# Second expert layer as split products of 384 and 256 columns, the feature chains shared by VectorE and GpSimd, class weights loaded behind the experts

## What is computed

```python
# 8 experts, top 2 of the softmaxed gate; token width D=192, hidden width F=768
logits = x @ gate_w + gate_b                     # [512, 8]
h = gelu(x @ w1[e] + b1[e])                      # for each expert e, 192 -> 768
y = h @ w2[e] + b2[e]                            # 768 -> 192
out = x + sum_e comb[:, e] * y_e + feat @ out_w  # comb: normalised weights of the top 2
# feat: two numbers a token, from a chain along the 64 tokens of an image
def bk_green_diag(a):                            # a: [batch, 64]
    d[n] = a[n] - 1.0 / d[n-1]                   # forward, 63 steps, one after the other
    e[n] = a[n] - 1.0 / e[n+1]                   # the same backward
    G = 1.0 / (d + e - a)
```

## Time and profile before

| | |
|---|---|
| Median of 3 runs | 411.57 us (411.3 to 412.5) |
| Profiled execution, its own time | 411.31 us |
| Its span in the trace | 409.6 us |
| TensorE busy | 384.5 us, 94% of the span |
| VectorE busy | 250.9 us, 61% |
| ScalarE busy | 174.7 us, 43% |
| GpSimd busy | 45.6 us, 11% |

### The profile page before, as it was taken

One profiled execution on the slowest core, in us unless ns is written; L12 is line 12 of the kernel. 1 busy time (PEld: TensorE's weight loads), 2 busy tenths in 40 slices (PEclk: granted clock), 3 DMA queues, 4 the chain that ended last, 5 costly groups with the idle time before them and its releaser, 6 DMA issues.

```text
span 409.6 us, 8771 instructions
## 1 busy us (share of the span) xinstructions
PE 384.5 (94%) x3602; PEld 315.0 (77%) x3602; DVE 250.9 (61%) x728; ACT 174.7 (43%) x304; POOL 45.6 (11%) x97
## 2 busy tenths in 40 slices
PE   8999999999877899999999989999999999999993
PEld 8988878788554657565548788998999899879783
DVE  1567766603497988888444487558458206677344
ACT  1256551842455565755435635235224310551420
POOL 7130010330000000100001400000000200304003
PEclk9999999999978999999999999999999989989999
DMA  7999500000289100000003996224401000000001
GB/s 194 258 223 252 118 9 2 2 0 0 61 229 272 53 2 2 2 2 3 2 0 87 280 265 162 77 60 134 130 9 56 2 0 2 2 2 2 0 2 38
DMA packets 28725, 30.69 MB, mean 75 GB/s; under 512 B 4867, under 2 KB 24137, under 8 KB 28686
## 3 DMA queue, kind: packets, MB, share of 16 engines
q1 hardware_dynamic: 28220, 29.96, 29.1%
q10 hardware_dynamic: 306, 0.17, 0.2%
q0 software_dynamic: 160, 0.01, 0.0%
HBM read 29.73 MB, written 0.39 MB: 74 GB/s over the span
## 4 chain that ended last, share of the span: by engine, by line
PE 73%; DVE 15%; ACT 5%; issue 2%; DMA 2%; POOL 2%; SPq 0%; DVEq 0%; POOLq 0%
PE ps L1510 66%; PE ps L1514 6%; DMA front<-in_x 2%; DVE front L1170 2%; DVE front L1171 2%; PE ps L1522 2%; DVE front L1179 1%; DVE front L1181 1%; DVE front L1164 1%; DVE bn L1015 1%; POOL rstd L524 1%; ACT front L745 1%; DVE front L1166 1%; DVE xn L1030 1%; DVE mv L1018 0%
## 5 line engine op out<-in xcount | busy, mean ns | idle before, releaser
L1510 PE MATMUL ps<-halves 128*128 128x512 f32 (+2 forms) x380 | 84.1, 376 | 1.3 <-ACT front L732 1.3
L1510 PEld LDWEIGHTS ps<-halves 128*128 128x128 f32 x380 | 66.5, 188 | 13.4 <-ACT front L732 1.7
L1510 PE MATMUL ps<-wide,front 128*128 128x192 f32 x432 | 73.7, 332 | 0.0
L1510 PEld LDWEIGHTS ps<-wide,front 128*128 128x128 f32 x432 | 72.0, 194 | 1.0 <-issue 0.5
L1510 PEld LDWEIGHTS ps<-front 64*32 64x32 f32 (+3 forms) x1488 | 52.0, 134 | 21.8 <-issue 9.4
L1510 PE MATMUL ps<-front 64*32 64x64 f32 (+3 forms) x1488 | 60.7, 245 | 8.1 <-ACT front L745 3.0
L732 ACT ACTIVATE front<-ps,colc 128x512 f32<-128x512 f32 x60 | 39.6, 690 | 52.3 <-PE ps L1510 52.2
L1313 DVE SCALAR_TENSOR_TENSOR xn<-ps,small,xn 128x192 f32<-128x192 f32 x28 | 9.7, 410 | 29.7 <-PE ps L1510 29.7
L1514 PE MATMUL ps<-ident,front 128*128 128x128 f32 x144 | 21.5, 286 | 6.5 <-DVE front L1181 5.3
L1514 PEld LDWEIGHTS ps<-ident,front 128*128 128x128 f32 x144 | 16.2, 144 | 10.2 <-DVE front L1181 7.2
L1510 PE MATMUL ps<-xT,turned 128*64 128x256 f32 (+1 forms) x96 | 23.4, 482 | 0.0
(11 more groups left out here) (280 smaller groups left out, 555.5 us busy)
## 6 DMA issues: line engine op xcount, KB each, us to landing
wide<-in_w SPq DMA_DIRECT2D x8, 576.0 KB, 4.7
wide<-in_w SPq DMA_DIRECT2D x8, 384.0 KB, 5.8
wide<-in_w SPq DMA_DIRECT2D x16, 192.0 KB, 6.3
front<-in_a2w SPq DMA_DIRECT2D x5, 576.0 KB
front<-in_a1w SPq DMA_DIRECT2D x5, 384.0 KB
front<-in_x SPq DMA_DIRECT2D x3, 512.0 KB, 7.9
front<-in_w_qkv SPq DMA_DIRECT2D x2, 576.0 KB, 7.7
front<-in_a1w SPq DMA_DIRECT2D x5, 192.0 KB
```

Of the source, the lines that this page charges most:

```text
L1510: return pe.matmul(o, l, r, start=start, stop=stop)
```

## The change

1. The second layer becomes split. ScalarE writes gelu's result to a scratch tile `hraw[f]`, then copies it to a high part (`hidden_high`); VectorE makes the low part (`hidden_low`). The second-layer weights get the same (`w2_high`, `w2_low`), high and low side by side, 384 columns. TensorE does, for each of 24 pairs of token and feature tile, one product of 384 columns and one of 256 (`down_split`). Its result takes all of banks 4 to 7, so there is one place in place of two, and adding it into `xn` takes eight instructions (`expert_in`).
2. The chains are shared. Of every 9 steps VectorE does 3 and GpSimd 6 (`CH_DVE, CH_ALL = 3, 9`), for experts 0 to 5; the last 9 steps, with expert 6, are VectorE's alone. A step on GpSimd is five instructions. The features are made with expert 6, not with expert 4.
3. On VectorE, `expert_in(e-1)` now stands behind `chain_part(e)` in the same turn of the loop, and behind `chains_end` and `features` in the turn of expert 6.
4. On TensorE the gate product is made ahead of the second half of the first `up`, and the exponential of the gate ahead of all gelus on ScalarE; the transposes for `combT` and the extra products move into the first layer of expert 7.
5. The memory of `a1w` and `a2w` now holds the split operands, so the class weights are loaded behind the experts: `a1w` after the second layer of expert 6, `a2w` after that of expert 7.

The diff, cut to what decides:

```diff
+CH_DVE, CH_ALL = 3, 9
@@ SyncE
-                    sp.wait_ge(s["y_mm"], e - NSLOT + 1)
+                    sp.wait_ge(s["w2_lo"], e - NSLOT + 1)
-                if e == NSLOT - 1:
...
+            sp.wait_ge(s["y_mm"], EM - 1)
+            sp.wait_ge(s["h_lo"], NF * EM)
+            for x in range(5):
+                for c, (r0, n) in enumerate(CH):
+                    load(a1w[0:n, x, c], a["a1w"][x, r0:r0 + n], "a_in")
+            sp.wait_ge(s["y_half"], 2)
+            for x in range(5):
+                load(a2w[:, x], a["a2w"][x].rearrange("(f p) n -> p f n", p=P), "a_in")
@@ GpSimd
+            def chain_step(n):
+                last = chS[:, n - 1, :]
+                link(pool.tensor_tensor(chr_[:, 0:2], last, last, ALU.mult))
+                link(pool.tensor_tensor(chr_[:, 2:3], chr_[:, 0:1], chr_[:, 1:2], ALU.add))
+                link(pool.tensor_tensor(chr_[:, 3:4], chr_[:, 2:3], chB[:, n, 1:2], ALU.pow))
+                link(pool.tensor_tensor(chr_[:, 0:2], last, chr_[:, 3:4].to_broadcast([16, 2]), ALU.mult))
+                return pool.tensor_tensor(chS[:, n, :], chr_[:, 0:2], chB[:, n, :], ALU.add)
+            for k in range(EM - 2):
+                pool.wait_ge(s["chain_dve"], k + 1)
+                for n in range(CH_DVE, CH_ALL):
...
+                tell(ins, "chain_pool")
@@ ScalarE
+            for e in range(EM):
+                for f in range(NF):
+                    expert_hidden(e, f)
+                    if f >= 1:
+                        hidden_high(e, f - 1)
+                hidden_high(e, NF - 1)
+                if e >= 1:
+                    w2_high(e)
                 if e + 2 < EM:
                     w1_high(e + 2)
@@ VectorE
+            def chain_part(e):
+                if e >= 1:
+                    dve.wait_ge(s["chain_pool"], e)
+                steps_here = CH_DVE if e < EM - 2 else CH_ALL
...
+            def expert_in(e):
+                dve.wait_ge(s["y_mm"], e + 1)
+                for i in range(NT):
+                    ins = weighted(xn, xn, e, i, 0)
+                link(ins)
+                for i in range(NT):
+                    ins = weighted(xn, xn, e, i, 1)
+                ins.then_inc(s["y_done"], 1)
+            for e in range(EM):
+                for f in range(NF):
+                    hidden_low(e, f)
...
+                if e >= 1:
+                    w2_low(e)
+                if e + 2 < EM:
+                    w1_low(e + 2)
                 if e == 0:
+                    chain_begin()
+                if e < EM - 1:
+                    chain_part(e)
+                if e == EM - 2:
                     chains_end()
                     features()
+                if e >= 1:
+                    expert_in(e - 1)
@@ TensorE
+            def down_split(e, tiles):
+                w, h = w2x[:, e % 2], hs[:, (e + 1) % 2]
+                for i in tiles:
+                    own = slice(i * P, (i + 1) * P)
+                    for f in range(NF):
+                        mm(ps[:, 4 + i, 0:2 * D], h[:, f, 0, own], w[:, f, :], f == 0, False)
+                        ins = mm(ps[:, 4 + i, 0:256], h[:, f, 1, own], w[:, f, 0:256], False, f == NF - 1)
+                return ins
...
+                else:
+                    up(w1x[e % 2], xs, range(2))
+                    pe.wait_ge(s["y_done"], e - 1)
                     for i in range(NT):
+                        ins = tr(ps[0:EM, 7, i * P:(i + 1) * P], comb[:, i, :])
                     ins.then_inc(s["combT_mm"], 1)
+                    up(w1x[e % 2], xs, range(2, 4))
+                    pe.wait_ge(s["combT_done"], 1)
                     pe.wait_ge(s["chF_in"], 32)
...
+                    up(w1x[e % 2], xs, range(4, NF))
+                    pe.wait_ge(s["extra_done"], 1)
                 if e >= 1:
+                    pe.wait_ge(s["w2_lo"], e)
+                    pe.wait_ge(s["h_lo"], NF * e)
+                    if e >= 2:
+                        pe.wait_ge(s["y_done"], e - 1)
+                    down_split(e - 1, range(NT)).then_inc(s["y_mm"], 1)
```

More of the change, by code:

```diff
@@ L224, in vit_tower @@
         a2w = take(5, NF, D)
+        halves_f = nc.alloc_sbuf_tensor_at("halves_f", [P, 22960], F32R, offset=front_at)
+        take = carve(halves_f)
+        hs = take(2, NF, 2, T)
+        raw_at = 2 * NF * 2 * T
+        take(3, T)
+        w2x = take(2, NF, 2 * D)
+        hraw = [turned[:, k * T:(k + 1) * T] for k in range(3)] + [
+            front[:, raw_at + k * T:raw_at + (k + 1) * T] for k in range(3)]
         take = carve(turned[:, xs_at + 4 * T:])
@@ L564, in _ @@
             pool.dma_start(chA[8:16], vrev.rearrange("o (b n) -> o b n", n=S)).then_inc(s["rowmv_in"], 16)
[L565 to L569, removed]
+            tell(pool.memset(wg2[0:DB], 0.0), "pad_made")
+            def chain_step(n):
[8 more added lines that the diff above has]
+                for n in range(CH_DVE, CH_ALL):
+                    ins = chain_step(1 + k * CH_ALL + n)
+                    if n < CH_ALL - 1:
+                        link(ins)
+                tell(ins, "chain_pool")
             pool.wait_ge(s["chain_in"], 2)
@@ L1252, in _ @@
                               ALU.subtract).then_inc(s["lg_sub"], 1)
+            w2_low(0)
             dve.wait_ge(s["lg_exp"], 1)
@@ L1329, in _, with hidden_low @@
                 ins.then_inc(s["y_done"], 1)
                 dve.wait_ge(s["y_done"], e + 1)
[L1331 to L1336 removed]
+            def hidden_low(e, f):
+                dve.wait_ge(s["h_hi"], NF * e + f + 1)
+                h = hs[:, (e + 1) % 2, f]
+                dve.tensor_tensor(h[:, 1, :], hraw[f], h[:, 0, :].bitcast(F32), ALU.subtract).then_inc(s["h_lo"], 1)
@@ L1797, in _, with up @@
             jobs = [0]
-            def up(w, x, tiles=range(NF), turn=0, hi="xs_hi", lo="xs_lo"):
+            def up(w, x, tiles=range(NF), turn=0):
                 for f in tiles:
@@ L2033, in gates, with value_row @@
                 pe.wait_ge(s["small_in"], 16 * 17)
+                for i in range(NT):
+                    for c in range(2):
+                        ins = mm(ps[:, 6, i * EM:(i + 1) * EM], xT[:, c, i * P:(i + 1) * P], gw[:, c, :],
+                                 c == 0, c == 1)
+                ins.then_inc(s["lg_mm"], 1)
+            def value_row():
                 for c in range(2):
@@ new lines, in _ @@
+            for e in range(EM):
+                pe.wait_ge(s["w1_lo"], e + 1)
+                if e == 0:
+                    up_high(w1x[0], xs, 0, nth(4, 0))
+                    up_rest(w1x[0], xs, 0, nth(4, 0))
+                    turn_part(xn, 1, 3, (4, 5))
+                    keep_busy(2, 6)
+                    part_ready(nth(4, 1))
+                    gates()
+                    up_high(w1x[0], xs, 1, nth(4, 1))
+                    up_rest(w1x[0], xs, 1, nth(4, 1))
+                    value_row()
+                    up(w1x[0], xs, range(4, NF))
+                elif e < EM - 1:
+                    up(w1x[e % 2], xs)
+                else:
+                    up(w1x[e % 2], xs, range(2))
+                    pe.wait_ge(s["y_done"], e - 1)
@@ L2081, in _ @@
+            pe.wait_ge(s["h_lo"], NF * EM)
+            pe.wait_ge(s["y_done"], EM - 1)
+            for g in range(2):
+                down_split(EM - 1, tiles_of(g)).then_inc(s["y_half"], 1)
+            turn_part(xn, 0, 4, (2, 5))
             keep_busy(3, 3)
```

221 lines of the change are left out of this document (84 added, 137 removed).

## The result

The changed kernel takes **447.34 us** (median of four runs, 445.07 to 447.70), the kernel before, on the same chip, 411.73 us: a ratio of 1.085, 95% interval 1.081 to 1.090. The prediction was 450.4 us, slower.

A forecast was written before the change was run, and what follows sets the result against it. TensorE, busy 94%, bounds the kernel; GpSimd's rounds of 17.3 us against its 14.3 would hold it. 411.3 + 37.4 (rounds and tail) + 1.7 (clock) = 450.4 us, range 422 to 468.

The forecast's parts named there:

- The mechanism: Experts' loop: GpSimd's share, lengthened by VectorE's subtractions, delays expert_in, which holds TensorE; with the tail, +37.4 us.
- rival 1: GpSimd is held up little or not, its share fits a turn, only the first round hurts: 428 us, chance 0.30.
- GpSimd's step: One chain step of five linked instructions on GpSimd: 1.85 us, six of them 11.1 us.
- The hold-up: VectorE's subtractions of two SBUF operands block GpSimd's instructions: some 4 us lost, making the share 15.2 us.
- The round: GpSimd's share, three VectorE steps and hand-over: 17.3 us against TensorE's 14.3, six rounds, the last 1.3 shorter.
- The second layer: Split products of 384 and 256 columns: 7.27 us an expert against 7.67, saving 3.2 us over eight experts.
- The start: Before expert 0's second layer: the 1.26 us gap goes, transposes move later, start at about 237.9 instead of 239.37.
- The tail: From expert 6's nine steps at 342.0 through features, additions and extra products to the first transposes at 385.3 against 347.95.
- The clock: TensorE's idle of some 15 us brings one more 1.2 GHz stretch on the path: +1.7 us, bounds 0 and 3.4.
- The class weights: Loads moved behind experts 6 and 7 cost nothing, first use some 35 us later, over 10 us of cover.
- 2 (485 us): GpSimd's small instructions cost 0.56 us like the long addition, about 23 us a round: 485 us, chance 0.06.
- 3 and 4: Added waits shrink below 5 us, so faster, 405 us, chance 0.03; or half the waits, 409 to 413, chance 0.04.

The follow-up runs named there:

- kernel with the memsets: Changed kernel with low parts of hidden values and second-layer weights zeroed by memset instead of VectorE's subtraction: 429.6 us (1.041).
- the two with the addition ahead: Changed kernel with expert_in(e-1) ahead of the chain steps in VectorE's queue, in every turn (440.7 us) or in expert 6's turn alone (443.8 us).
- second rearranged kernel: Changed kernel with chain shares, addition, features, transposes and extra products reordered, then W1's low parts behind expert_in and 8, 6, 6, 6, 6, 6, 5 VectorE steps: 409.44 us.
- rearranged kernels: Changed kernel with new chain shares and tail order: 411.17 us; with two further edits: 409.44 us; with eight filler products added to those: 414.72 us.

## Why the prediction was right, point by point

- **The mechanism** was right, its four links too: share, `expert_in` behind it, TensorE, and the tail. The kernel with the memsets shows the first link, the two with the addition ahead that the order mostly decides who waits. (Where the prediction speaks of "the second case below", its rival 1 is meant.)
- **The first chain steps** were put at 239.5 and stood at 239.4.
- **GpSimd's step**: 1.85 predicted, 1.68 measured beside an idle VectorE (249.14 to 250.82 in the first round), 1.67 beside its addition (257.77 to 259.44). The term that was mis-sized is mainly the small instruction: 0.22 from a two-element row, 0.18 to 0.19 in fact; the power took 0.54 for 0.57. Six steps are 10.1, not 11.1.
- **The hold-up**: 4 us predicted, 14.1 - 10.1 = 4.0 measured. The count behind it was off: the prediction speaks of eleven or so subtractions in a turn, the program has nine (six `hidden_low`, one `w2_low`, two of `w1_low`); the instructions that got through beside them were at the short end of what it allowed, and the product came out. The share was 14.1 instead of 15.2.
- **The round**: 17.3 predicted, 16.1 measured, nearly all of it from GpSimd's step. The nine steps of expert 6 started at 335.1 instead of 342.0. The waits ahead of the second layers were so 6.86 us at first, then 0, 1.85, 0.48 and 2.03, not about 3 each. Where one is missing, TensorE had used the time itself, at the slow clock behind a gap: the second layer at 260.63 took 9.71 us.
- **The second layer**: 0.4 us an expert predicted, 0.63 measured. 384 columns were interpolated at 0.179; the pair of 384 and 256 takes 7.04 / 24 = 0.293, so if 256 columns are 0.124, 384 are 0.169.
- **The start**: second layer of expert 0 predicted at 237.9, measured at 239.76. The gap did go, but the clock was at its 1.2 GHz level from 225.1 to 228.5 and one group took 4.14 us instead of 2.64, and the trace was 0.7 us late at the stage's start. In the second rearranged kernel, where the clock stayed up, the layer starts at 237.97.
- **The tail**: the pieces came as laid out. Nine steps and `chains_end` 335.1 to 340.9, the DMA until 343.08, features until 345.47, `expert_in(5)` until 348.3; that is 13.2 us, as predicted. The wait at `combT` was 1.45 for 1.8, at `extra_done` 0.75 for 2.0, at `expert_in(6)` 3.00 for 3.1.
- **The clock**: +1.7 predicted, bounds 0 and 3.4. This is the step that failed, the one term that lay outside its bounds. From the restart at 348.33 to the end of expert 6's second layer at 373.4 it took 25.1 us, not 18.9: two stretches at 1.2 GHz (337.7 to 351.4 and 354.8 to 368.4) instead of one of 3.4 us. On the path that is +6.2, where +1.7 was put down: 7.7 by the long rows of the tail, less 1.6 by which the waits at `combT` and `extra_done` were shorter. That the forecast came within 1% is partly luck: 6.9 us too many in the rounds stood against 4.5 too few of clock.
- **The class weights**: nothing predicted, nothing found, by the kernel before with late loads and by the changed kernel's memory traffic, where they come from 374 to 395 us and no engine's wait in the trace is for a DMA.
- **The rivals**: 1 (GpSimd not held up, 428 us) is close to what the kernel with the memsets gives when most of the hold-up is taken away, 429.6. 2 (485 us) falls with the small instruction at 0.18 to 0.19 us, not 0.56. 3 and 4 needed the added waits to shrink below 5 us or to half; together they did so only in the rearranged kernels.

## What to carry over

Work that is off the bound engine isn't free when a third party's queue has it ahead of the bound engine's next input: price the round of the helper, with what the other engine's two-operand instructions do to it, against the round of the bound engine. If it is longer, moving the consumer ahead mostly moves the wait (here it won 6.6 of 36 us); a smaller share, or another order of the whole tail, is what helps. And give idle time of TensorE two prices, one for itself and one for the slower clock that came with most of the longer waits here.

## What the runs showed of the hardware

- Tiny instructions of GpSimd (16 x 1 and 16 x 2 elements) are 0.18 to 0.19 us beside an idle or PSUM-reading VectorE, a power 0.54, 0.08 between linked ones; beside VectorE's subtractions of two SBUF operands, 0.63 to 1.36 us each, up to 1.19 and 1.26. In the kernel with the memsets one took 1.99.
- In the changed kernel the granted clock was at 0.50 for stretches of about 3.4, 10.2 and 13.7 us. That of 10.2 began 2 us into a standstill of 6.86 us, the first of 13.7 began 3 us into one of 13.68 us, the second among the extra products, 0.7 us after a wait of 1.45. A wait of about 2 us was followed by a fall behind the restart at 292.87 (1.85) and by none at 325.10 (2.03); at 225.1 the clock fell without any wait. Which of these come is not something that the traces of this case allow to foretell.
- A pair of split products of 384 and 256 columns takes 0.293 us, thirty of 512 columns 6.83 to 6.97.
